# Two more pairs' second copies sent during attention, and one shared pair moved from ahead of the expert tiles to behind them

## What is computed

```python
h = concat(patch_tokens, hashed_text)            # 64 x 229 x 128
h = h + attn(layernorm(h))
t = layernorm(h)                                 # 14656 rows
shared = sum over 2 shared experts of gelu(t @ sw1 + sb1) @ sw2 + sb2
probs = softmax(t @ gate_w.T + gate_b)           # 8 experts
top_v, top_i = top_k(probs, 2)
routed = sum over the 2 chosen of top_v * (gelu(t @ rw1[e] + rb1[e]) @ rw2[e] + rb2[e])
out = h + shared + routed
```

## Time and profile before

| | us |
|---|---|
| median of 3 runs | 1250.35 |
| lowest and highest | 1245.68, 1252.9 |
| the profiled execution, its own time | 1243.88 |
| span in its trace, first to last instruction | 1242.2 |

### The profile page before, as it was taken

How to read it: one execution, slowest core, us unless ns; L and a number is a source line. 1 busy time by engine, 2 the same in 40 slices (tenths; PEclk the granted TensorE clock), 3 DMA queues, 4 the chain that set the end, 5 groups by cost and what they waited for, 6 DMA issues and landing times.

```text
span 1242.2 us, 32105 instructions
## 1 busy us (share of the span) xinstructions
PE 1169.7 (94%) x9514; PEld 886.8 (71%) x9514; DVE 970.1 (78%) x2516; ACT 807.6 (65%) x1867; POOL 840.9 (68%) x808
## 2 busy tenths in 40 slices
PE   4999999999999999868999988999999999999998
PEld 2777777777777777644555447999999889964555
DVE  5688898888888888757987765777777767778997
ACT  2566666666665566535555545777777777768877
POOL 4435776666677776546887784777777777776564
PEclk8999999999999999979999998999999999999999
DMA  6233444444444442223444424544555444439998
GB/s 179 81 113 115 129 132 132 131 132 126 119 134 128 131 121 74 67 73 101 112 114 128 111 62 88 98 97 99 93 95 92 92 97 96 90 81 189 204 201 165
DMA packets 208056, 143.53 MB, mean 116 GB/s; under 512 B 119036, under 2 KB 186745, under 8 KB 207892
## 3 DMA queue, kind: packets, MB, share of 16 engines
q1 hardware_dynamic: 166868, 93.93, 30.1%
q0 software_dynamic: 36992, 40.97, 15.4%
q10 hardware_dynamic: 4032, 6.57, 2.1%
HBM read 70.38 MB, written 55.96 MB: 102 GB/s over the span
## 4 chain that ended last, share of the span: by engine, by line
PE 33%; POOL 32%; issue 24%; SPq 4%; DMA 3%; ACT 3%; DVE 1%; POOLq 0%; ACTq 0%; DVEq 0%
POOL slots_dram L483 9%; POOL slots_dram L1544 4%; POOL y_dram L1555 4%; POOL rstd L524 3%; PE bank L1832 3%; PE bank L1856 3%; PE bank L1857 3%; PE bank L1855 3%; PE bank L1834 3%; PE bank L1833 3%; PE bank L1263 2%; POOL rstd L530 2%; PE bank L1264 2%; PE bank L1265 2%; PE bank L1304 2%
## 5 line engine op out<-in xcount | busy, mean ns | idle before, releaser
L1555 POOL DMA_INDIRECT y_dram<-y_sb,y_row x244 | 268.3, 1100 | 92.7 <-issue 74.1
L1640 ACT ACTIVATE gel_all<-bank,b 128x256 f32<-128x256 f32 x488 | 191.8, 475 | 49.7 <-PE bank L1834 47.7
L1271 ACT ACTIVATE gel_all<-bank,b 128x458 f32<-128x458 f32 x256 | 154.8, 640 | 83.5 <-PE bank L1265 56.2
L1855 PE MATMUL bank<-w_part_hi,hid_all 128*128 x976 | 170.5, 219 | 0.0
L1857 PE MATMUL bank<-w_part_hi,hid_all 128*128 x976 | 169.9, 219 | 0.0
L1856 PE MATMUL bank<-w_part_lo,hid_all 128*128 x976 | 169.9, 219 | 0.0
L1762 DVE CAST hid_all<-gel_all 128x1024 f16<-128x1024 f32 x122 | 85.6, 702 | 107.0 <-ACT gel_all L1640 107.0
L483 POOL DMA_INDIRECT slots_dram<-row_bufs,slot_1st x128 | 129.9, 1015 | 39.2 <-issue 39.2
L1764 DVE TENSOR_TENSOR hid_all<-gel_all,hid_all 128x1024 f16<-128x1024 f32 x122 | 149.5, 1225 | 4.2
L1544 POOL DMA_INDIRECT slots_dram<-row_bufs,slot_2nd x104 | 125.6, 1208 | 31.6 <-issue 31.0
L1282 DVE TENSOR_TENSOR hid_all<-gel_all,hid_all 128x916 f16<-128x916 f32 x128 | 142.4, 1113 | 4.4
(11 more groups left out here) (190 smaller groups left out, 3001.8 us busy)
## 6 DMA issues: line engine op xcount, KB each, us to landing
xin<-in_xmain SPq DMA_DIRECT2D x32, 771.8 KB
x2r_dram<-row_bufs SPq DMA_DIRECT2D x32, 260.0 KB, 2.1
x2t_dram<-x2T SPq DMA_DIRECT2D x32, 229.0 KB, 2.9
row_bufs<-x2r_dram SPq DMA_DIRECT2D x26, 260.0 KB, 2.9
x_cols<-x2t_dram ACTq DMA_DIRECT2D x28, 229.0 KB, 2.8
stage<-in_ffn_w SPq DMA_DIRECT2D x20, 256.0 KB
xin<-in_xrest SPq DMA_DIRECT2D x32, 128.6 KB
y_dram<-y_sb,y_row POOLq DMA_INDIRECT x244
```

The costliest lines, as they stand in the source:

```text
L1271: act.activation(self.gel[:, f // 2 % 2, f % 2, :], self.up_dst(k, f), ACT.Gelu, bias=self.b1[:, f:f + 1]).then_inc(self.gel_ready, 1)
L1555: pool.indirect_dma_start(out=y_dram, in_=y_sb[:, s, c, :], in_offset=None, out_offset=bass.IndirectOffsetOnAxis(ap=y_row[:, s, c:c + 1], ...
L1640: act.activation(gel[:, s8 % 2, f, :], up_bank[s8 % 2][half][:, (f % 2) * TILE:(f % 2 + 1) * TILE], ACT.Gelu, bias=of_expert(b1, SHARED * ...
L1855: pe.matmul(part, h_hi, w2_hi, start=False, stop=False)
```

## The change

`AGAIN` goes from 6 to 8, and a list gives for each of these pairs the step of its load and its buffer: pairs 0, 1 and 2 at steps 11, 14 and 17 in buffer 0, pair 3 at step 20 in buffer 1, then 22, 24, 26 and 28 in buffers 0, 1, 0, 1. Waits that counted buffers by `k % 2` now count by the list. The exponential of the tags (ACT) and the difference ahead of it (DVE) move from steps 17 and 16 to steps 10 and 9, and cover 32 columns where they covered 24. 24 pairs are left for the second stage. `EARLY_PAIRS` goes from 18 to 17, and so `LATE_PAIRS` from 14 to 15, and `combined` spreads 30 sums over 26 halves where it spread them over 24.

```diff
-AGAIN, AGAIN_AT = 6, 18
+AGAIN_STEPS = ((11, 0), (14, 0), (17, 0), (20, 1), (22, 0), (24, 1), (26, 0), (28, 1))
+AGAIN = len(AGAIN_STEPS)
...
-EARLY_PAIRS = 18
+EARLY_PAIRS = 17
...
         def again(i):
 
-            k, second = divmod(i - AGAIN_AT, 2)
-            return (k, second) if 0 <= k < AGAIN else (None, second)
+            for k, (at, buf) in enumerate(AGAIN_STEPS):
+                if i - at in (0, 1):
+                    return k, i - at
+            return None, 0
+
+        def again_buf(k):
+
+            return AGAIN_STEPS[k][1]
+
+        def again_uses(k):
+
+            return sum(buf == again_buf(k) for at, buf in AGAIN_STEPS[:k])
...
             def load_again(k):
 
-                if k == 1:
+                if again_buf(k) == 1 and again_uses(k) == 0:
                     sp.wait_ge(ws_done, WBLOCKS)
                 if k > 0:
                     sp.wait_ge(tagged, k)
-                if k > 1:
-                    sp.wait_ge(again_out[k % 2], 64 * (k // 2))
+                if again_uses(k) > 0:
+                    sp.wait_ge(again_out[again_buf(k)], 64 * again_uses(k))
                 sp.wait_ge(r_out[k % ROW_BUFS], 16 * (k // ROW_BUFS + 1))
-                sp.dma_start(rows_again[k % 2], x2r_dram[k]).then_inc(again_in, 16)
+                sp.dma_start(rows_again[again_buf(k)], x2r_dram[k]).then_inc(again_in, 16)
...
-                if i == AGAIN_AT - 2:
+                if i == AGAIN_STEPS[0][0] - 2:
...
-                if i == AGAIN_AT - 1:
+                if i == AGAIN_STEPS[0][0] - 1:
...
-            slot, first = 2 * k + half, 4
-            per = (PAIRS - 2) / (2 * LATE_PAIRS - first)
-            return range(int(per * max(slot - first, 0)), int(per * max(slot - first + 1, 0)))
+            slot, slots = 2 * k + half - 4, 2 * LATE_PAIRS - 4
+            return range((PAIRS - 2) * max(slot, 0) // slots, (PAIRS - 2) * max(slot + 1, 0) // slots)
```

More of the change, by code:

```diff
@@ L493, in scatter_again @@
                     pool.indirect_dma_start(
-                        out=slots_dram, in_=rows_again[k % 2][0:m, c, :], in_offset=None,
+                        out=slots_dram, in_=rows_again[again_buf(k)][0:m, c, :], in_offset=None,
                         out_offset=bass.IndirectOffsetOnAxis(ap=slot_2nd[0:m, 4 * k + c:4 * k + c + 1], axis=0)
-                    ).then_inc(again_out[k % 2], 16)
+                    ).then_inc(again_out[again_buf(k)], 16)
             def sum_biases(n):
@@ L989, in tag_again @@
                 act.wait_ge(again_in, 16 * (k + 1))
-                act.activation(rows_again[k % 2][:, :, HID:], tag_2nd[:, 4 * k:4 * k + 4, :], ACT.Copy).then_inc(tagged, 1)
+                act.activation(rows_again[again_buf(k)][:, :, HID:], tag_2nd[:, 4 * k:4 * k + 4, :], ACT.Copy).then_inc(tagged, 1)
             steps(act, step, PAIRS - 1)
@@ L1457, in sync_between @@
         def sync_between(sp):
-            sp.wait_ge(done.again_out[0], 64 * uses(0, 2, AGAIN))
+            sp.wait_ge(done.again_out[0], 64 * sum(buf == 0 for at, buf in AGAIN_STEPS))
             for k in range(2):
@@ L1513, in sync @@
                 sp.wait_ge(scattered[b], 64 * uses(b, ROWS_BUFS, PAIRS - AGAIN))
-            sp.wait_ge(done.again_out[1], 64 * uses(1, 2, AGAIN))
+            sp.wait_ge(done.again_out[1], 64 * sum(buf == 1 for at, buf in AGAIN_STEPS))
             for t in range(TILES):
```

## The result

| | before | with the change |
|---|---|---|
| median of 20 runs each, us | 1250.19 | 1247.01 |
| lowest and highest | 1245.39, 1255.23 | 1242.59, 1251.94 |
| profiled execution, its own time | 1243.88 | 1245.23 |
| its span | 1242.2 | 1243.4 |

The ratio is 0.9974 with a 95% interval of 0.9961 to 0.9986. That is 3.2 us faster (1.8 to 4.9), and clear of noise, though less than 0.5%. The forecast was +0.8 us, no change: the time is within the range, the direction is not the one forecast.

The account below looks back on a forecast made before the run. PE was busy 1169.7 of 1242.2 us; the gain was PE's standing time ahead of the tiles, set by POOL's scatters. -12.1 + 3.4 + 9.5 = +0.8 us on 1250.35 gave 1251.2 us, range 1244.0 to 1258.0.

Parts of the forecast that it names:

- Term 1, POOL's end: Ahead of the tiles: eight scatters leave POOL's stage at 1.512 us each, so its last scatter starts 12.1 us earlier.
- Term 2, the seam: Ahead of the tiles: PE ends 9.74 us earlier, still waits for POOL, gap 4.4 us instead of 6.7; no cost itself.
- The rival in which PE sets it: Ahead of the tiles: PE is late, tiles start only 9.7 us earlier, +3.2 us in all, 1253.6 us; chance 0.10.
- Term 3, attention: Inside attention: scatters beside the split delay POOL's powers in five new steps at 0.68 us, +3.4 us; bounds 0 to 8.2.
- Term 4, the late pair: Behind the tiles: a fifteenth pair costs 9.83 us, two doubled halves fewer give 0.36 back, +9.5 us; bounds 9.2 to 10.01.
- much less than 9 us: Sign set in advance behind the tiles: the prediction is wrong if the last stage grows by much less than this.
- Hidden late pair: Rival, last stage: DMA for the sums sets the pace, the added pair costs nothing, -8.7 us, 1241.7 us; chance 0.12.
- Full price beside the split: Rival, attention: each scatter pair costs its full 2.5 us in five steps, +9.9 us in all, 1260.3 us; chance 0.12.
- The clock behind the seam: At the first tiles: loads, not slow matmuls, set the pace; full clock gives at most 0.7 us, kept for the range.

Follow-up runs that it names:

- d4: The change itself, run once more unaltered: 1247.06 us against 1250.91 for the kernel before, ratio 0.9972.
- a2: The change but with 18 early pairs, so eight pairs in attention and no shared pair moved: 1239.77 us against 1251.41 before, ratio 0.9923.
- a1: The change with only six pairs, in steps 11, 14, 17, 20, 22 and 24, and 18 early pairs: 1253.35 us against 1251.41 before.
- b1: a2 with SP waiting for the last early down matmul before the first tile load: 1252.03 us against 1252.05 before, ratio 1.0002.
- b3: a2 with the second sum of a doubled half put into its pair's first half: 1238.05 us against 1252.05 before, ratio 0.9897.
- a3: The shared pair alone: the change with the six pairs at before's steps, 17 early and 15 late pairs: 1257.23 us against 1251.41 before.
- b2: a2 with POOL's second-copy scatters moved ahead of the split of weights: 1235.61 us against 1252.05 before, ratio 0.9877.
- d1: The change (17 early pairs) with POOL's second-copy scatters moved ahead of the split of weights: 1245.15 us against 1250.91 before, ratio 0.9938.
- c2: a2 with the edits of b2 and b3 together, on a slow chip: ratio 1.0055 to the kernel before, which took 1435.71 us there.
- d2: a2 with the edits of b2 and b3 together, on a chip like the earlier ones: 1231.49 us against 1250.91 before, ratio 0.9854.

## Why the prediction was wrong

- **Term 1, POOL's end: right.** -12.1 forecast, -12.13 in the ledger.
- **Term 2, the seam: right.** POOL still sets it; a gap of 4.4 us forecast, 4.29 found. That the number fits so well is luck: in d4, the same kernel, it is 1.85, with a slow stretch (granted clock 0.79 in 705 to 710 us) in the early pairs. The rival in which PE sets it is what a2 is, not the change.
- **Term 3, attention: the mechanism right, the size too large.** 3.4 us were forecast for five steps at 0.68. By the lags, steps 12 and 13 cost 1.40 together, 15 and 16 another 1.22, and step 18, which stands next to the step 19 that before pays for too, only 0.15: 2.8 in all. What failed beyond that is the assumption that these steps are the whole of it: from step 28 to 29 the change takes 15.83 us where before takes 17.49, since a stretch at 1.2 GHz is missing. That makes +1.04 instead of +3.4. The stretch is missing in all six profiles with the scatters of this change behind the split (a1, a2, b1, b3, d4, the change) and there in both with before's steps (before, a3), but b2 and d1 show that one and the same code can go either way, so that it is not shown what the change has to do with it. I had read the clock only at the seam, not at attention's end.
- **Term 4, the late pair: too large.** +9.5 forecast, +7.3 found (d4: 7.7), by the prediction's own mark ("much less than 9 us") a sign of being wrong. I took the spacing behind a doubled half, 9.83, for that of a plain pair; the plain one is 9.74. I priced a doubled half at 0.18, from one interval instead of the two that it touches; it costs 0.36. And I counted doubled halves (six to four) without looking at which half: the two that went to first halves cost nothing, so four went, not two. 9.74 - 4 x 0.36 = 8.3, and that is what the stage has grown by when its first interval is left out (138.4 us before, 146.6 to 146.7 in the change, a3 and d4). The other 1.0 is mostly that interval, 10.28 in place of 11.20 us, where ACT waits 2.7 in place of 3.6 us for the first sum. It varies with the profile, from 9.74 (a1, d1) to 11.46 (b2), and is 10.67 in d4, so that this part is chance.
- **The sum.** With the two terms as found, 1.0 - 12.1 + 0.1 + 7.3 = -3.7 us. Both errors, 2.4 and 2.2 us, went the same way and turned the sign. With only what the edits are shown to do, 2.8 in attention and 8.3 behind the tiles, the sum is -12.1 + 2.8 + 0.1 + 8.3 = -0.9 us: the sign turns even so, but most of the measured 3.2 us is the missing slow stretch (1.7) and what varies between executions.
- **The rivals.** Hidden late pair: out (a3). Full price beside the split: out (a1). One argument for it was wrong: that no scatter can be slipped into POOL's 2.68 us wait for ACT holds only for the order of this change, and b2 puts the scatters there. The clock behind the seam: the reading from the rows, that the slow matmuls cost next to nothing there, held. d4 has a granted clock of 1.00 in 735 to 745 us and takes 12.41 us from tile 0's first matmul to tile 4's; before, with its slow stretch, takes 11.94, and a2, whose loads lead by 8 us, 10.65.
- **What the prediction did not see at all.** In the chain of waits PE's gap at the seam looked like the whole price of being late. It is not: the head start of the loads that goes with it is worth about as much again (5.7 us of tiles between a2 and before, 8.8 between a2 and the change, against 6.7 of gap). The change pays a shared pair to make PE early at a seam that POOL then still sets, and so gives back most of what two more pairs in attention had won (a2 against the change: -9.6 and -3.2 us).

## What to carry to other kernels

When work leaves the engine that sets a seam, don't also take work from the one that waits there: a consumer that arrives a little late lets the loads run ahead, and where issue is about as slow as consumption that head start is what absorbs late issues for the whole stage. Work that is slipped into a busy engine's order costs nothing where that engine waits and its full chain where others wait behind it, so look for the wait in the step itself and put the work ahead of it. Price a repeated disturbance over all the intervals that it touches, and check in which position it stands.

## What the runs showed of the hardware that was not expected

- A pair of loads (transpose 1.21 us, tags 0.42 us on SP's queue) takes 2.6 us of SP at best and 2.82 on the mean in before, about as long as a tile's 2.78 us of matmuls. With 2 us of head start the 122 tiles took 344.5 to 352.0 us in eight profiles, with 8 us or more 338.7 to 339.1 in six.
- The same sparse stretch of matmuls was followed by a stretch at 1.2 GHz in d1 (granted clock 0.66 in 510 to 515 us) and by none in b2 (1.00), with the same code and a start 0.4 us apart; the step took 17.48 and 15.82 us.
- One chip took 1435.71 us for the kernel that takes 1250 to 1252 on the others, and there all three versions were 0.5 to 0.7% slower than before; one of them is 1.5% faster than before on another chip (c2 and d2 are one kernel).
